# Transformer decoder block on one core: the transposed row maxima in one block, added by selector products

## The reference

```python
# 1: attention, 16 heads of 8 channels; Q and K also see a 3-tap convolution
q_in = x @ Wq.T + b;  Q = concat(q_in, conv3(q_in)) @ qproj.T + b      # K likewise
tau   = sigmoid(conv1(gelu(depthwise_conv3(x))))      # per head and query
delta = sigmoid(conv1(gelu(depthwise_conv3(x))))      # per head and key
scores = (Q @ K.T) / sqrt(8) * tau[..., None] + delta[:, :, None, :]
x = layernorm(x + (softmax(scores) @ V) @ Wo.T + b)
# 2: gated attention against ctx, 4 heads of 32 channels, causal, with
#    D = exp(cumulated log forget gates + input gate - its row maximum)
C = (q @ k.T) / sqrt(32) * D
h = C / (max(|sum C|, exp(-max)) + 1e-6) @ v;  x = layernorm(x + norm(h) * (1 + w))
# 3: linear layer on block-quantised values (blocks of 32, FP6 grid)
x = layernorm(x + dequant(quant(x)) @ dequant(quant(W)).T + bias)
```

## Time and profile before

| | us |
|---|---|
| median of 3 runs | 238.55 (237.43 to 240.87) |
| the profiled execution | 238.0 |
| its span, first to last instruction | 236.3 |
| TensorE busy | 208.4 (88%) |
| VectorE busy | 154.1 (65%) |
| ScalarE busy | 134.2 (57%) |
| GpSimd busy | 132.0 (56%) |

### The profile page before, as it was taken

One profiled execution on the slowest core, in us unless ns is written; L12 is line 12 of the kernel. 1 busy time (PEld: TensorE's weight loads), 2 busy tenths in 40 slices (PEclk: granted clock), 3 DMA queues, 4 the chain that ended last, 5 costly groups with the idle time before them and its releaser, 6 DMA issues. The chain is left out here.

```text
span 236.3 us, 5909 instructions
## 1 busy us (share of the span) xinstructions
PE 208.4 (88%) x2217; PEld 132.0 (56%) x2217; DVE 154.1 (65%) x354; ACT 134.2 (57%) x346; POOL 132.0 (56%) x239
## 2 busy tenths in 40 slices
PE   1799889699999999899888899789889969699895
PEld 1676454244566455566546567366648756276552
DVE  4587889959444553557647779966684475556871
ACT  2632867556854643673763768757776465515332
POOL 7994629691232192581695848862781757523520
PEclk9997999979999999999999999999997967899799
DMA  5822110000000000202002003003002003000001
GB/s 145 206 37 78 47 47 0 1 0 3 0 3 3 0 3 1 92 3 81 11 1 94 3 1 115 0 25 97 23 0 67 28 8 103 3 22 1 22 1 47
DMA packets 10220, 8.40 MB, mean 36 GB/s; under 512 B 1872, under 2 KB 9264, under 8 KB 10192
## 3 DMA queue, kind: packets, MB, share of 16 engines
q1 hardware_dynamic: 8816, 7.83, 11.2%
q0 software_dynamic: 512, 0.18, 0.7%
q10 hardware_dynamic: 864, 0.01, 0.2%
HBM read 6.94 MB, written 1.08 MB: 34 GB/s over the span
## 5 line engine op out<-in xcount | busy, mean ns | idle before, releaser
L996 DVE TENSOR_REDUCE nm<-score 128x8 f32<-128x1024 f32 x32 | 39.1, 1223 | 22.0 <-PE score L740 22.0
L511 ACT ACTIVATE prob<-score 128x1024 f32<-128x1024 f32 x32 | 32.6, 1021 | 21.2 <-PE score L755 21.0
L740 PE MATMUL score<-km,qf 32*128 32x512 f32 x128 | 35.0, 640 | 0.8 <-ACT prob L511 0.7
L750 PE MATMUL score<-qm,kf 32*128 32x512 f32 x128 | 35.0, 639 | 0.8 <-DVE nm L996 0.8
L775 PE MATMUL pvb<-ones 128*128 128x512 bf16 x80 | 23.5, 436 | 0.0
L359 POOL CAST nmx<-nm 128x16 bf16<-128x16 f32 x16 | 4.1, 254 | 30.4 <-DVE nm L996 30.4
L381 POOL TENSOR_TENSOR u<-u,maskb 128x1024 f32<-128x1024 f32 x7 | 16.5, 2358 | 7.2 <-DMA u<-gates_out 7.2
L768 PE MATMUL pvb<-prob,vz 128*32 128x128 f32 x512 | 17.4, 277 | 2.2 <-ACT prob L511 2.2
L859 PEld LDWEIGHTS qkb<-ctm,cc 128*128 128x128 f32 x128 | 15.3, 194 | 4.3 <-issue 2.2
L768 PE MATMUL pvb<-prob,ez 128*32 128x128 f32 x512 | 16.9, 273 | 0.0
L859 PE MATMUL qkb<-ctm,cc 128*128 128x33 f32 x128 | 15.7, 278 | 1.3 <-DVE cc L1069 0.8
(11 more groups left out here) (248 smaller groups left out, 485.8 us busy)
## 6 DMA issues: line engine op xcount, KB each, us to landing
u<-gates_out SPq DMA_DIRECT2D x7, 512.0 KB, 3.7
xt<-in_x_dram SPq DMA_DIRECT2D x4, 256.0 KB, 4.3
cin<-in_ctx_dram SPq DMA_DIRECT2D x4, 256.0 KB, 3.4
out_dram<-th SPq DMA_DIRECT2D x8, 128.0 KB, 1.9
ck<-in_L_attn_convk_w_dram SPq DMA_DIRECT2D x1, 192.0 KB, 3.6
cq<-in_L_attn_convq_w_dram SPq DMA_DIRECT2D x1, 192.0 KB, 3.9
pk<-in_L_attn_kproj_w_dram SPq DMA_DIRECT2D x1, 128.0 KB, 2.9
pq<-in_L_attn_qproj_w_dram SPq DMA_DIRECT2D x1, 128.0 KB, 3.4
```

What stands on the lines that cost most here:

```text
L511: nc.scalar.activation(prob[:, n % 2, 2 * h:2 * h + 2, :].rearrange("p g s -> p (g s)"), sc[:, 1024 * h:1024 * (h + 1)], ACT.Exp, scale=0. ...
L740: ins = mm(sc[:, 512 * q:512 * (q + 1)], qf[r, n, :], km[r, n % (2 * CB)].rearrange("p j s -> p (j s)"), start=True, stop=True)
L750: mm(sc[:, 512 * q:512 * (q + 1)], kf[r, m, :], qm[r, m % (2 * CB)].rearrange("p j s -> p (j s)"), start=True, stop=False)
L996: nc.vector.tensor_reduce(nm[:, n % RING, 8 * h:8 * (h + 1)], sc[:, 1024 * h:1024 * (h + 1)].rearrange("p (h s) -> p h s", h=8), AX_X, ALU ...
```

## The change

- `nmx` and `nmT` hold one block of 128 columns per batch. Column 32g + 4s + j is part s of the maximum of head j in row group g; before, each head j had a block of its own. The other columns stay zero.
- One transpose (128 x 128) in place of four, and a copy of 128 columns in place of 512.
- The product with ones, 512 columns wide, becomes four products of 128 columns per row group, each with a selector `sel[:, j, :]`, whose rows are one where the row's number modulo 4 is j. The selectors are built once, by VectorE, in the stage `vzero`; TensorE waits for them ahead of the first use.
- A place of `warm` makes one unread product instead of two, and has 80 places instead of 40.
- PLACES is another table on all engines.

```diff
 PLACES = {
-    "tx": (0, 6, 8, 12), "wab": (1,), "wm": (2, 3), "ww": (4, 9), "wt": (5,), "pk": (7, 26, 60, 67),
+    "tx": (0, 6, 9, 13), "wab": (1,), "wm": (2, 3), "ww": (4, 10), "wt": (5,), "pk": (7, 20, 22, 27),
...
-        mcol = sb("mcol", [P, J]);
+        mcol = sb("mcol", [P, J]); msel = sb("msel", [P, J]); sel = sb("sel", [P, J, P], BF16)
...
-        nmx = sb("nmx", [P, RING, J * (S + 1)], BF16)
-        nmT = sb("nmT", [P, RING, J * S], BF16)
+        nmx = sb("nmx", [P, RING, P], BF16)
+        nmT = sb("nmT", [P, RING, S], BF16)
...
-                    v = nm[:, n % RING, :].rearrange("p (g j) -> p j g", j=J)
-                    rv = nr[:].rearrange("p (j g) -> p j g", j=J)
-                    x3 = nmx[:, n % RING, :].rearrange("p (j c) -> p j c", j=J)
-                    hi, mid, lo = (x3[:, :, J * s:J * s + 3 * 32 + 1:32] for s in range(3))
+                    v = nm[:, n % RING, :].rearrange("p (g j) -> p g j", j=J)
+                    rv = nr[:].rearrange("p (g j) -> p g j", j=J)
+                    x3 = nmx[:, n % RING, :].rearrange("p (g c) -> p g c", g=G)
+                    hi, mid, lo = (x3[:, :, J * s:J * (s + 1)] for s in range(3))
...
-                    nc.scalar.activation(nmT[:, n % RING, :], trb[:, 0:J * S // 2].bitcast(BF16), ACT.Copy).then_inc(nmT_sb, 1)
+                    nc.scalar.activation(nmT[:, n % RING, :], trb[:, 0:S // 2].bitcast(BF16), ACT.Copy).then_inc(nmT_sb, 1)
...
                         pe.wait_ge(nmT_sb, m + 1)
-                        for q in (2 - 2 * h, 3 - 2 * h):
-                            r = slice(32 * q, 32 * (q + 1))
-                            ins = mm(sc[:, 512 * q:512 * (q + 1)], ones[r, :], nmT[r, m % RING, :], start=False, stop=True)
+                        if k == 0:
+                            pe.wait_ge(vzero, 1)
+                        for j in range(J):
+                            for q in (2 - 2 * h, 3 - 2 * h):
+                                r = slice(32 * q, 32 * (q + 1))
+                                ins = mm(sc[:, 512 * q + S * j:512 * q + S * (j + 1)], sel[r, j, :], nmT[r, m % RING, :], start=False, stop=(j == J - 1))
...
-                    for k in range(2):
-                        mm(pvb[:], ones[:], ones[:].unsqueeze(1).to_broadcast([P, 512 // P, P]), start=True, stop=True)
+                    mm(pvb[:], ones[:], ones[:].unsqueeze(1).to_broadcast([P, 512 // P, P]), start=True, stop=True)
...
-                    for j in range(J):
-                        ins = nc.tensor.transpose(trb[:, 0:J * S // 2].bitcast(BF16)[:, S * j:S * (j + 1)],
-                                                  nmx[:, n % RING, S * j:S * (j + 1)], identb[:])
-                    ins.then_inc(nmT_ps, 1)
+                    nc.tensor.transpose(trb[:, 0:S // 2].bitcast(BF16), nmx[:, n % RING, :], identb[:]).then_inc(nmT_ps, 1)
...
-                    nc.vector.memset(vz[:], 0.0).then_inc(vzero, 1)
+                    nc.vector.memset(vz[:], 0.0)
+                    link(nc.vector.tensor_reduce(msel[:], ident[:].rearrange("p (a j) -> p j a", j=J), AX_X, ALU.max))
+                    nc.vector.tensor_copy(sel[:], msel[:].unsqueeze(2).to_broadcast([P, J, P])).then_inc(vzero, 1)
```

## The result

The changed kernel takes 248.13 us (median of 4 runs, 247.63 to 250.50) against 237.99 for the kernel before on the same chip: a ratio of 1.046, 95% interval 1.036 to 1.055. It is slower by 4.6%; forecast were 234.8 us and a range up to 241.5. The profiled execution took 247.81 us (span 246.1), that of before 238.0 (span 236.3), so 9.8 us are to be found. (Some executions of every kernel here are disturbed; ratios with an interval leave those out, medians and ranges of runs do not.)

What follows compares the result with a forecast made beforehand. TensorE was taken as the bound from about 57 us on; -3.8 - 0.5 + 2.9 - 3.0 + 0.7 = -3.7 us from 238.0 gives 234.3, with 0.5 to the median 234.8 us; range 229.5 to 241.5.

Steps and rivals of the forecast that it cites:

- What bounds the kernel: Whole program: TensorE is the bound from about 57 us on; before that it is not.
- the work that is done early: Projections and a transposition moved ahead of 63 us: TensorE work, counted in full wherever done; part of the -3.0 us.
- One transpose for four: Transposes of the split maxima on TensorE: 0.24 us less in each of 16 batches, -3.8 us.
- Short copy: ScalarE's copy of the transposed block, 128 columns for 512: shorter way to the PSUM bank's next user, -0.5 us.
- Selector products: Eight short products for two wide ones, each of 32 halves: 0.09 us more per half, +2.9 us.
- Rival 2: Every half phase: selector products do not overlap, costing 12.5 instead of 2.9 us, so 244.4 us; chance 0.1.
- rival 1: Between 80 and 160 us: TensorE waits give back the early work, all 3.0 us lost, 237.8 us; chance 0.15.
- First 60 us: New order at the start, walked: 3.9 us ahead at 63.8, less hand-overs, -3.0 us, bounds 0 and -3.9.
- Rival 4: A wait in the new start lets the clock fall: 3.5 us, so 238.3 us; chance 0.08.
- Last 50 us: Unread products placed singly, and z3 ahead of the last bn_stats on VectorE: together +0.7 us, bounds 0 and +1.5.
- signs of being wrong: Selector products over 0.2 us more per half, or TensorE idle over 7 us between 120 and 160.
- signs of being right: New profile: transpose, selector and copy times, TensorE over 18.5 of 20 us early, third k projection 38-40, x2 1 us later.

Runs made afterwards that it cites:

- e17: Changed kernel with unread products filling six TensorE waits: ahead of the first three cell products and three short waits around the third; 242.57 us, ratio 1.017.
- e1: Selector products, single transpose and short copy in the order of the kernel before, unread products in pairs again; 235.75 us, ratio 0.992.
- e18: The changed kernel, unchanged, run once more for a second profile; 249.65 us, ratio 1.044.
- e15: Changed kernel with the third and fourth k projections moved back behind the second and third value products; 259.50 us.
- e6: Changed kernel with nine unread 512-column products in TensorE's wait ahead of the third pair's cell product; 246.03 us, ratio 1.030.
- e5: Changed kernel with GpSimd's two passes over the second pair's decay matrix cut to one of 16 rows of heads; 246.99 us (238.07-247.33).
- e13: Changed kernel with unread products in all four TensorE waits around the third pair's cell product; 245.04 us.
- e8: New form with the new order up to the first selector products and the old order for the rest; 248.79 us, ratio 1.049.
- e14: e1 with one unread VectorE reduction of 2048 columns ahead of the third pair's gate sums; 239.33 us.
- e10: Changed kernel with ten unread products at the start and nine ahead of the third cell product; 243.91 us, ratio 1.013.

## Why the prediction was wrong, by its steps

- **What bounds the kernel.** Right that TensorE is the bound from the first subtraction on. The step that failed is what follows from it in the text, that "the work that is done early" behind 63 us "counts in full wherever it is done". It takes the clock for given. Over 60:180 TensorE is busy 111.0 us before, 109.0 in the changed kernel and 113.0 in e17, nearly the same; what is done in that time differs by the clock, 0.99, 0.91 and 1.00.
- **One transpose for four, -3.8.** Right by the row: 0.07 us each for 0.08 forecast. **Short copy, -0.5**: the copy takes 268 ns as forecast; what that gave TensorE no run shows by itself.
- **Selector products, +2.9.** Mis-sized. They measure 0.32 us for eight against 0.31 for two, so 32 x 0.01 = +0.3 us, at the lower bound that the text kept. The chain of 0.05 + 3 x 0.08 us within a row group was my error: the float products at 105.00 in the earlier trace rows, 0.041 us each, were the right row, and four per group and half fit into it (8 x 0.041 = 0.33). The load rule of the Trainium skill (TensorE: Matmul & The Clock Gate, LDWEIGHTS (loading the stationary operand)) taken alone is the case of 0.64 us for the eight; the trace agrees with that page's The mechanism, in Part 3, instead. Rival 2 is refuted.
- **The form in sum.** With the right price -3.8 - 0.5 + 0.3 = -4.0; measured in e1 -1.9 (interval of the ratio -0.7 to -3.4 us). By the pages of before and e1, TensorE's work shrank by 2.7 and its waiting grew by 2.5, and between the first and the thirtieth subtraction 0.7 us are gained. That is rival 1's mechanism, met by the form and not by the early work. The prediction counted each microsecond taken off TensorE in full.
- **First 60 us, -3.0.** Failed. The walk holds to within 0.1 us up to the q projection at 35.59. It then has k 2 at 38.3; it came at 40.29, after 1.89 us of waiting for VectorE's addition to kf. Further waits are 0.57 us for the tanh at 51.87 (forecast 0 to 0.2) and 0.43 at 56.47. The third half is at 58.93 instead of 56.2. The walk followed TensorE's order and took VectorE's at the place where it suited; but VectorE stood before the addition with two taps lengthened to 0.96 and 1.06 us (37.49 to 39.54) behind 1.40 us of waiting for ScalarE. Its "longest wait 0.6" was 1.89. B0 was 5.5 us later than before, and 9.2 in e18's execution. The bound "0 if a wait that I overlooked" was too near: it priced a wait once, and not that the chain of three engines comes late as a whole. The projections that are done early there are worth their place all the same (e15).
- **Rival 4, the clock.** Right mechanism, wrong place and price. It was put into the start at 3.5 us, with 0.08. It came behind the third pair's cell product, for 13.6 us, and is worth 6.5 to 7.1 us in all (e17, e18), 5.3 to 5.5 of them behind that one wait (e6, e18): the largest part of the loss. The prediction followed the new table for 60 us and not at all beyond; the gate sums of the third pair, which it moves from ahead of GpSimd's passes to beside them, stand in that part.
- **Rival 1** was priced at 3.0 us with GpSimd and VectorE half idle as the reason against it. Their share of busy time says nothing about whether one holds up the other.
- **Last 50 us, +0.7.** Measured +0.1. The two operations changed places as forecast; the last bn_stats starts at 235.30 and x2 at 237.13, 1.83 us later, where it was 1.91 before, so the order costs nothing there:

```profile
234.96 0.42 DVE L1140 TENSOR_TENSOR abT<-yb,x2b 128x256 f32<-128x256 f32 x1 [0.96 <-PE yb L871]
235.30 0.48 DVE L1122 BATCH_NORM_STATS2 st<-z 128x6 f32<-128x128 f32 x2
...
237.13 0.69 DVE L1105 TENSOR_SCALAR x<-z,mv,rs 128x128 f32<-128x128 f32 x2 [1.07 <-ACT rs L439]
```

- **What was to show it.** Neither of the two signs of being wrong came: TensorE idles 5.4 us between 120 and 160, under the 7 of the text, and the selector products cost next to nothing. Three of the signs of being right did fail, in the start and at the end: TensorE is busy 18.08 of 20 us in 20:40 for over 18.5, the third k projection is at 40.29 for 38 to 40, and x2 of the last pair is no further from its z. The granted clock in the same rows was the sign, and the text looked for it only up to 60 us.

What stays open: the part of about 4 us (1.7%) that the new order costs with the clock held. The start is later by 5.5 to 9.2 us, and some of it is given back: in e5's profile B0 is 5.3 us later than in the kernel before and the last subtraction 1.0, in e13's, where the wait of 2 us is filled and not gone, 5.8 and 3.2. Which VectorE or ScalarE operation has to move is not known, since e8 and e15 each made another wait. Why three runs of e5 took 247 us is open too; no profile shows them. A kernel with the old start and the new rest was not run.

## What to carry to other kernels

Judge an order of work by the waits that it leaves on TensorE, with the clock in view: a wait of 2.3 us cost 5.3 us beyond its own length here, since 13.7 us of half clock followed it (e18, e6), while one of 3.35 us in front of large products cost 4.0 in all, of which 1.7 were clock (e14). Where such a wait can't be removed, products that nobody reads are an easy test and may be a remedy: 28 of them gave back 2.7%. What is taken off the busiest engine can turn into waiting: by the rows the form took 4.0 us off TensorE, and it gave 1.9. Follow a new order on all engines and to the end, above all where a small VectorE operation comes to stand beside a long GpSimd pass, and compare a kernel's profile in more than one execution before a stretch of it is explained.

## What the runs showed of the hardware

- VectorE operations on 8 or 16 numbers per partition, 0.17 us as a rule, took 1.34 and 1.85 us beside GpSimd passes of 2.38 and 1.91 us, and ended with them; one between the two passes (L1083) and one behind them (L1025) took 0.17. In e5, with the passes cut to one row of heads, the two took 0.17 and 0.18 us and the wait behind them was gone. The Trainium skill (SBUF — State Buffer, Who interferes with whom) has a port pair that VectorE and GpSimd share and lock for a whole instruction; the trace agrees. The price here was not the 2.9 us of VectorE alone but the clock of TensorE behind them.
- The clock differed between executions of one program: half clock at 90 to 97 us in one profile of the changed kernel and at 108 to 112 in the other, and, by the durations of the products (0.88 or 1.62 us for two of 384 columns), the first rise before 12.2 us or after 20. The late one moved the first subtraction by 3.7 us. The row of the granted clock does not show a low clock ahead of its first change: it says 1.00 there.
- Behind waits of 0.77, 0.59 and 0.73 us between short products, with full work before them, the clock fell in e10 and held in e6; of the five profiles with such waits and no longer one ahead of them it fell in three, for 6.8 us each.
- Eight bf16 products of 128 columns with a load each, in two row groups of 32, take 0.32 us together, 0.04 us each.
